# Three-pass products that read their moving columns, and write their outputs, in descending order

## The reference

```
x = x + attention0(convolution(x))     # 32 heads of width 128, causal softmax
x = x + octonion_ffn(conditioning(x))  # conditioning: 512x512 weight, bias, a LoRA of rank 32
x = x + attention1(adapter(x))         # adapter: 512x512 weight, bias, a LoRA of rank 16
x = x + moe(routed(x))                 # top-2 LoRA experts, then sparsemax LoRA experts

attention0:  q, k, v = h @ wq, h @ wk, h @ wv
             out = softmax(causal(q @ k.T * scale)) @ v @ wo
adapter:     h = x @ W.T + b + (x @ A[id].T) @ B[id].T
```

## The kernel before

| Stage | calls of 512 columns | calls of 256 columns |
|---|---|---|
| attention, queries and keys | 896 | |
| attention, values | | 896 |
| attention, output | 512 | |
| conditioning | 96 | |
| second layer | 196 | 64 |
| all | 1700 | 960 |

## Time and profile before

### The profile page before, as it was taken

The page is one execution under the profiler, slowest core; times in us unless marked ns, Lnnn a source line. Parts: engine busy times, 40 slices in busy tenths (PEclk is TensorE's granted clock), DMA queues, the critical chain, the costliest instruction groups (busy, mean ns, idle before and its releaser), DMA issues. The chain is left out here.

```text
span 2126.5 us, 36954 instructions
## 1 busy us (share of the span) xinstructions
PE 2094.1 (98%) x11922; PEld 1813.5 (85%) x11922; DVE 1386.8 (65%) x2619; ACT 718.8 (34%) x1444; POOL 1256.7 (59%) x1315
## 2 busy tenths in 40 slices
PE   7999999999999999999999999999999999999999
PEld 5888888888898898989888898989887778878887
DVE  8767777676767777665666566565756766655444
ACT  5333232332323232332323233323323744443332
POOL 3578585777767676767758576776746642114220
PEclk9999999999999999999999999999999999999999
DMA  7421212111111226211111211111112200001110
GB/s 241 154 60 48 53 48 83 54 51 48 49 52 44 61 61 205 83 41 41 40 39 39 69 49 39 40 39 39 40 61 78 89 20 0 0 1 40 39 39 20
DMA packets 122616, 122.28 MB, mean 58 GB/s; under 512 B 35250, under 2 KB 101458, under 8 KB 120498
## 3 DMA queue, kind: packets, MB, share of 16 engines
q1 hardware_dynamic: 91697, 109.87, 16.7%
q10 hardware_dynamic: 29568, 7.34, 1.7%
q0 software_dynamic: 1280, 4.20, 0.7%
HBM read 108.13 MB, written 13.28 MB: 57 GB/s over the span
## 5 line engine op out<-in xcount | busy, mean ns | idle before, releaser
L215 PE MATMUL psum<-yc,wh 128*128 128x512 f32 x904 | 360.5, 399 | 0.3 <-PEq L264 0.3
L217 PE MATMUL psum<-yc,wh 128*128 128x512 f32 x904 | 352.4, 390 | 0.0
L216 PE MATMUL psum<-yc,wh 128*128 128x512 f32 x904 | 352.2, 390 | 0.0
L215 PE MATMUL psum<-kept,yc 128*128 128x256 f32 x896 | 255.4, 285 | 6.5 <-DVE u L1415 5.8
L1466 DVE TENSOR_TENSOR resid<-psum,resid 128x512 f32<-128x512 f32 x248 | 171.3, 691 | 134.6 <-PE psum L217 129.0
L217 PE MATMUL psum<-kept,yc 128*128 128x256 f32 x896 | 251.5, 281 | 0.0
L216 PE MATMUL psum<-kept,yc 128*128 128x256 f32 x896 | 251.5, 281 | 0.0
L1017 POOL TENSOR_TENSOR wh<-wh_f,wh 128x256 fp32r<-128x256 f32 x256 | 189.7, 751 | 103.9 <-ACT wh L983 102.0
L1017 POOL TENSOR_TENSOR wh<-raw,wh 128x256 fp32r<-128x256 f32 x192 | 142.3, 741 | 99.9 <-ACT wh L983 99.9
L217 PEld LDWEIGHTS psum<-yc,wh 128*128 128x128 f32 x904 | 169.7, 188 | 35.9
L215 PEld LDWEIGHTS psum<-yc,wh 128*128 128x128 f32 x904 | 170.1, 188 | 31.5 <-issue 0.7
(11 more groups left out here) (367 smaller groups left out, 4930.6 us busy)
## 6 DMA issues: line engine op xcount, KB each, us to landing
raw<-in_attn_w SPq DMA_DIRECT2D x96, 512.0 KB, 5.0
wo_f<-in_attn_w SPq DMA_DIRECT2D x31, 512.0 KB, 4.0
hankel<-kernel_rows SPq DMA_DIRECT2D x32, 256.0 KB, 4.8
y_parts<-stage ACTq DMA_DIRECT2D x56, 128.0 KB, 2.3
yc<-y_parts SPq DMA_DIRECT2D x7, 1024.0 KB, 5.1
resid<-in_xT SPq DMA_DIRECT2D x4, 1024.0 KB, 9.7
outT<-wide SPq DMA_DIRECT2D x16, 256.0 KB, 2.6
kept_f<-in_l_w SPq DMA_DIRECT2D x3, 1024.0 KB, 5.8
```

Source lines behind the costliest of these rows:

```text
L215: pe.matmul(out, w[0], x[0], start=start, stop=False)
L216: pe.matmul(out, w[0], x[1], start=False, stop=False)
L217: return pe.matmul(out, w[1], x[0], start=False, stop=stop)
```

## The change

`mm3` reverses the order of the columns before it issues its three matmuls: the moving operands and the output are given with a step of -1 instead of 1 along the free dimension. Column 511 (or 255) is read and written first, column 0 last. The stationary operand is as before. Since input and output are reversed alike, each result lands at the same address as before.

More of the change, by code:

```diff
@@ L213, in mm3 @@
         def mm3(pe, out, w, x, start, stop):
+            out, x = out[:, ::-1], (x[0][:, ::-1], x[1][:, ::-1])
             pe.matmul(out, w[0], x[0], start=start, stop=False)
```

## The result

| | before | after |
|---|---|---|
| median of 4 executions | 2126.83 us | 2152.49 us |
| lowest and highest | 2125.39 to 2128.37 | 2151.05 to 2153.93 |
| span of the profiled execution | 2126.5 us | 2150.2 us |

The ratio is 1.0121, with a 95% interval of 1.011 to 1.0133: the changed kernel is slower by 25.7 us. The forecast was no change.

A forecast was written before the change was run, and what follows sets the result against it. The prediction took PE to bound the kernel; a change of 0 us on the 2126.5 us span, with 1.8 us around it, gave 2128.3 us profiled, forecast as a median of 2127.7 us. The range was 2091 to 3531 us.

The forecast's parts named there:

- The bound: Whole kernel: PE sets the time, busy 2094.1 of 2126.5 us, so a matmul step's change goes in nearly one for one.
- the gaps: PE's idle time from 62 us on, 19.6 us: at most some 20 us of a loss could disappear there.
- the count: Three-pass products: 5100 matmuls with 512 columns and 2880 with 256, 7980 together, are reversed.
- The share of the second layer's slower step: Second layer: its 588 wide passes add some 2 us, also given as 588 x 6.9 ns = 4 us, to present time.
- 7980 x 0 ns: All reversed passes keep their ascending steps of 226.4 and 118 ns: 0 us on 2126.5 us of span.
- Its reason: Operand access in reversed passes: neighbours stay adjacent and memory serves the same number of lines, so change is 0 ns.
- a fixed cost per pass: Rival: each descending row's beginning or end costs a few ns more; at 6.9 ns 55 us, 2183 us; chance 0.11.
- Half pace: Rival: every `mm3` pass falls to one column in two cycles, price 1315 us, time 3423 to 3531 us; chance 0.24.
- partial loss: Rival: one further cycle per pair of columns in the reversed passes, 698 us, 2826 us in all; chance 0.04.
- a loss beyond half pace: Rival: the reversed passes get slower than half pace; no size given; chance 0.04.
- the gain: Rival: the excess of reversed passes over one column a cycle shrinks, to 2054 us, or 2091 at half; chance 0.07.
- the likeliest case: No change in the steps of the reversed passes, 2123 to 2133 us; chance 0.50.

The follow-up runs named there:

- e10: All three-pass products read and write groups of 4 columns ascending, the columns inside each group descending, against the kernel before: 2128.59 us, ratio 1.0002.
- e11: All three-pass products read and write groups of 4 columns descending, the columns inside each group ascending, against the kernel before: 2152.15 us, ratio 1.0111.
- e2: Only the output of the three-pass products written descending, moving columns read ascending, against the kernel before: 2128.79 us, ratio 1.0005.
- e6: Kernel before plus 34 groups of 48 matmuls behind its last product, varying read order, row start and block width; from start 128: 226.7 ns ascending, 233.3 descending.
- e8: Kernel before, all ascending, with the output projection's moving rows 32 bytes further on, starting at 160 modulo 256: 2133.40 us, ratio 1.0037.
- e3: Kernel before plus 47 groups of 12 matmuls behind its last product, varying row start, block start and order: ascending 227 to 235 ns, descending 233 to 236.7.
- e7: Kernel before plus 44 groups of 48 passes behind its last product, rows read in chunks, order reversed between or inside chunks: 226.7 to 266.7 ns for 512 columns.
- e15: Kernel before plus 24 pairs behind its last product, 24 passes of some kind, then 48 of a target: narrow targets 113.3 or 117.8 ns, wide 226.7.

## Why the prediction was wrong

**The bound, the gaps and the count were right.** PE set the time. The cost was borne by its step from start to start, and the gaps took up a few us (4.9 in the attention), within the 20 that were allowed. The share of the second layer's slower step is given once as 2 and once as 4 us; 588 x 6.9 ns is 4, and the forecast does not use it.

**The step that failed** is "The value that I take is the nearest row, the same passes ascending: 226.4 and 118 ns, a change of 0 ns." The term 7980 x 0 ns should have been some 28 us: 4512 x 6.1 = 27.5 us for the wide passes of attention and conditioning, 588 x 1.6 = 0.9 us for those of the second layer, and about 0 for the 2880 narrow ones. PE's stages show 24.9 + 2.0 + 0.9 = 27.8 us of it. In the attention 4.9 us went into gaps, in the second layer PE was idle for 0.8 us more, and 23.7 us are left in the span.

**Its reason was half right.** "Any group of 2 or 4 neighbouring float32 columns is still visited one right after the other" is true and is indeed free (e10). "The same number of lines, only from the other end" is true too, but the number is not all that counts: lines taken downward cost 6.6 ns a pass where lines taken upward, with row and block at the same start, do not (e11). The working treated PE's excess of 13 ns over one column a cycle as a constant of the pass. It is a state, and 226.7 ns is the quick one.

**The sign was in rows 6.** One shape had 226.4 ns in one stage and 233.3 in another, and the second is the very step to which the descending passes went. The working used the row for a rival, "a fixed cost per pass" at 6.9 ns, which had the size for a wide pass (6.6). It gave 2183 us because it charged all 7980 passes. Had it asked which passes could be slowed to the step that the second layer already has, it would have charged the 4512, 31 us at 6.9 ns, and come to about 2159 us. That would have hit the size without the cause: the second layer is slow because its rows and most of its blocks start at different places.

**The other rivals.** Half pace did not occur: 233 ns, not 430. The reading of the Trainium skill ("Advanced Engine Details and Errata", Memory Cachelines) by which a non-contiguous PSUM pattern slows matmuls significantly does not hold for a step of -1: e2 writes 7980 passes so at a ratio of 1.0005. The same section's reason for SBUF, that accesses to the line already open run at full performance, agrees with e10; it says nothing of the order of lines, which is what e11 measured. The partial loss of 698 us, a loss beyond half pace and the gain did not occur either. The range of 2091 to 3531 us held the time, but the own range of the likeliest case did not, and the direction was missed.

**What stays open.** Shown are the side (read), the grain (16 bytes), that the quick step goes with a row and a block that start at the same place (with the exceptions named above), and for narrow passes the dependence on entry. Not shown is the memory mechanism behind it. The rows are consistent with a moving read and a weight load that must keep out of each other's way in SBUF, since the quick step depends on the places of both, but the width of the block did not act as that theory said (e6).

## What to carry to other kernels

Take the step from start to start of the bounding engine's instructions for each shape in each stage before predicting. If one shape has two steps, the quicker one can be lost by an edit that changes no work. Reverse a moving operand only within 16 bytes or in large blocks, and write a reversed output freely. Before moving or padding tensors of a kernel bound by float32r matmuls, let each row start at the same place modulo 256 bytes as the block that it meets: 32 bytes between them cost this kernel 0.4% (e8).

## What the hardware showed that was not expected

- A 512-column float32r pass with a block of 128 columns has a few steady steps: 226.7 ns, 228.9 ns, 232 to 235 ns, up to 236.7 ns for some descending rows (e3), and 266.7 ns where groups of 16 columns are read backward inside (e7). A 256-column pass lies between 113.3 and 120.0 ns, most often at 113.3, 117.8 or 120.0.
- The quick step of 226.7 ns of a wide pass goes with a row and a block that start at the same place modulo 256 bytes: 227.4 ns against 232 to 234.5 ns among passes of one shape in one stage of the kernel before.
- Which of its steps a narrow pass takes can depend on the passes before it, for at least 48 passes on (e15).
- A descending read has no quick start: 233.3 ns from all eight starts (e6).
- Plain float32 at two cycles a column (429 ns for 512) pays nothing for descending order: 20.76 us for 48 records both ways (e6).
